# Layer 2's last node stage made block by block inside its second edge pass

## The reference, cut to what matters

```
for i in range(LAYERS):                               # LAYERS = 2
    x1 = _gat_layer(x1, src, dst, W, a_s, a_d, concat=i != LAYERS - 1)   # 8 heads, softmax over edges
    x2 = _rel_gcn_layer(x2, src, dst, edge_weight, gcn_params[i])        # relu of a weighted mean
return jnp.maximum(x1, x2)
...
h = jnp.maximum(_layernorm(x), 0.0)
x = x + _L2_gnn_ref(h, ...)
h = jnp.maximum(_layernorm(x), 0.0)
x = x + _L3_gnn_ref(h, ...)       # 9 steps h <- norm * A h, summed with softmax weights, then a product
```

## Time and profile before

| | us |
|---|---|
| median of 3 runs | 2660.73 |
| lowest, highest | 2654.13, 2671.45 |
| the profiled execution, its own time | 2652.48 |
| its span | 2650.7 |
| granted TensorE clock, mean over the span | 0.783 of full |
| busy: PE, DVE, ACT, POOL | 2346.3, 1452.3, 1208.4, 1198.2 |

### The profile page before, as it was taken

One profiled execution on the slowest core, in us unless ns is written; L12 is line 12 of the kernel. 1 busy time (PEld: TensorE's weight loads), 2 busy tenths in 40 slices (PEclk: granted clock), 3 DMA queues, 4 the chain that ended last, 5 costly groups with the idle time before them and its releaser, 6 DMA issues.

```text
span 2650.7 us, 51792 instructions
## 1 busy us (share of the span) xinstructions
PE 2346.3 (89%) x12833; PEld 1958.4 (74%) x12833; DVE 1452.3 (55%) x6161; ACT 1208.4 (46%) x5256; POOL 1198.2 (45%) x1268
## 2 busy tenths in 40 slices
PE   3778778787549999999899999999979999999998
PEld 2555556554339999999857777777878899888887
DVE  5656556578536666666436566665564333344443
ACT  3666667675313333333314343343674444444443
POOL 3777777700067777775077777775131000000000
PEclk9856566588755555555698697888899999999999
DMA  3242442431244444443244344443272000000002
GB/s 90 61 125 64 123 125 64 125 103 42 66 111 113 110 109 108 109 110 106 53 110 110 100 111 108 109 108 85 68 283 83 14 22 18 25 25 25 25 25 61
DMA packets 172291, 227.45 MB, mean 86 GB/s; under 512 B 63503, under 2 KB 131160, under 8 KB 171736
## 3 DMA queue, kind: packets, MB, share of 16 engines
q0 software_dynamic: 50176, 131.74, 18.8%
q1 hardware_dynamic: 114350, 88.60, 11.1%
q10 hardware_dynamic: 7466, 3.73, 0.5%
HBM read 183.63 MB, written 40.29 MB: 84 GB/s over the span
## 4 chain that ended last, share of the span: by engine, by line
PE 71%; issue 7%; DVE 7%; POOL 5%; ACT 4%; DMA 4%; ACTq 2%; DVEq 0%; SPq 0%; POOLq 0%
PE banks L2644 10%; PE banks L2640 10%; PE banks L1675 7%; PE banks L1733 7%; PE banks L1734 6%; POOL arena L229 5%; PE banks L1736 4%; PE banks L1739 3%; PE banks L2646 3%; PE banks L733 2%; PE banks L945 2%; PE banks L1737 2%; DMA arena<-h_table,arena 2%; PE banks L736 2%; PE banks L1691 1%
## 5 line engine op out<-in xcount | busy, mean ns | idle before, releaser
L229 POOL DMA_INDIRECT arena<-value_table,arena x392 | 387.2, 988 | 318.2 <-DMA ed_table<-arena 199.1
L2640 PE MATMUL banks<-counts,u_parts 128*128 128x448 f32 x1323 | 491.7, 372 | 9.6 <-DVE u_parts L2771 9.6
L2644 PE MATMUL banks<-counts_even,u_parts 128*128 128x448 f32 x1323 | 486.3, 368 | 0.0
L229 POOL DMA_INDIRECT arena<-gat_table,arena x392 | 392.2, 1001 | 207.3 <-issue 88.0
L229 POOL DMA_INDIRECT arena<-h_table,arena x392 | 376.3, 960 | 119.4 <-issue 88.4
L2819 DVE CAST counts_even<-counts 128x448 fp32r<-128x448 bf16 x450 | 163.9, 393 | 304.1 <-PE banks L2644 276.1
L733 PE MATMUL banks<-arena 128*128 128x425 bf16 x392 | 198.3, 506 | 84.6 <-ACT arena L789 77.5
L2640 PEld LDWEIGHTS banks<-counts,u_parts 128*128 128x128 f32 x1323 | 249.6, 189 | 30.3 <-issue 9.7
L736 PEld LDWEIGHTS banks<-arena 128*128 128x128 f32 x784 | 211.1, 293 | 80.9 <-issue 72.7
L2644 PEld LDWEIGHTS banks<-counts_even,u_parts 128*128 128x128 f32 x1323 | 249.5, 189 | 20.7 <-ACT counts_even L2747 0.2
L1675 PE MATMUL banks<-arena 128*128 128x256 bf16 (+1 forms) x967 | 262.8, 370 | 1.7 <-DVE arena L2250 1.7
(11 more groups left out here) (301 smaller groups left out, 4758.5 us busy)
## 6 DMA issues: line engine op xcount, KB each, us to landing
adj_rows<-arena SPq DMA_DIRECT2D x5, 4000.0 KB
counts<-adj_rows SPq DMA_DIRECT2D x2, 7200.0 KB, 21.6
arena<-ed_table SPq DMA_DIRECT2D x784, 0.5 KB
arena<-turned_rows SPq DMA_DIRECT2D x27, 448.0 KB, 3.4
arena<-h_table,arena POOLq DMA_INDIRECT x392
arena<-value_table,arena POOLq DMA_INDIRECT x392
arena<-gat_table,arena POOLq DMA_INDIRECT x392
counts<-adj_rows SPq DMA_DIRECT2D x2, 1600.0 KB, 6.2
```

Of the source, the lines that this page charges most:

```text
L229: return e.indirect_dma_start(into, None, table, bass.IndirectOffsetOnAxis(ap=index.bitcast(U32), axis=0))
L2640: e.matmul(banks[:, 2 * r, 0:HALFW], weight, C_odd[:, w0:w0 + HALFW], start=start, stop=stop)
L2644: x = e.matmul(banks[:, 2 * r + 1, 0:HALFW], weight, tile(n), start=start, stop=stop)
```

## The change

Blocks 0 to 22 are now made inside the second edge pass. Block b begins eight chunks after its last chunk, at c0 = block_end(b) + 8. In the seven chunks c0 to c0 + 6 the fillers are left out, and bank 7, in which they were written, takes the block's weight sums and products in three parts (three heads at c0, four at c0 + 3, one and the convolution at c0 + 5). ACT scales each part back into the accumulator's own columns (at its chunks c0 + 2, + 4, + 6), DVE turns the weight sums into factors at c0 + 2 and adds all at c0 + 8, normalization follows every fourth block. The factor 1/8 moves from the scales into the weights. x is loaded and stored four blocks at a time behind the gather ring; the normalized rows go to places in the accumulators that are no longer needed (`home`). Only blocks 23 and 24 stay in `layer2_end`. Count blocks 0, 2, ..., 12 are asked for when 20 blocks are normalized, 18 to 23 at the last edge product, the odd ones after the last block's addition, then 24, and 14 and 16 in the diffusion. `weights_t` spreads one row (the last step's) in place of ten.

```diff
@@ -1436,7 +1436,7 @@
-def layer2_edges(i, begin):
+def layer2_edges(i, begin, nodes):
...
@@ -1507,7 +1508,13 @@
     def sp(e):
         begin(e)
         first = Windows(e, FI, f"e2w_{i}")
+        if i:
+            nodes.begin_sp(e)
         for b in range(NBATCH):
+            if i:
+                for g in nodes.sp_at(b):
+                    nodes.x_store(e, g)
+                    nodes.x_load(e, g + 1)
             if b >= RE:
                 e.wait_ge(e2_bd, nb0 + b - RE + 1)
             first.load(b * BC)
...
+            for b in range(NBATCH, NBATCH + 8):
+                for g in nodes.sp_at(b):
+                    nodes.x_store(e, g)
+                    nodes.x_load(e, g + 1)
...
@@ -1637,13 +1649,27 @@
+        if i:
+            nodes.begin_dve(e)
         for p in range(NBATCH + 4):
+            if i and p == 1:
+                nodes.degrees(e)
             for q in range(SLOTS):
                 c = chunk_at.get(SLOTS * p + q)
                 if c is not None:
                     spread(c)
                     if c % PER == 1 and c > 3 * PER:
                         share(c // PER - 2)
+                    if i:
+                        for b, c0 in nodes.first.items():
+                            if c == c0 + 2:
+                                nodes.weigh(e, b)
+                            if c == c0 + 8:
+                                nodes.summed(e, b)
+                                if b % 4 == 3 and b < 20:
+                                    nodes.variances(e, b // 4)
+                            if c == c0 + 12 and b % 4 == 3 and b < 20:
+                                nodes.scales(e, b // 4)
...
@@ -1746,7 +1772,13 @@
                     busy(512, 512, 512)
                 if c is not None:
                     sums(c)
-                    busy(512, 256)
+                    if not i or c not in nodes.waiting:
+                        if i and c - 1 in nodes.waiting:
+                            nodes.bank_free(e, (c - nodes.first[0]) // BC // 2)
+                        busy(512, 256)
+                    else:
+                        for b, k in nodes.pe_at(c):
+                            nodes.products(e, b, k)
...
@@ -1830,6 +1864,14 @@
                         keep_shared(c // PER - 1)
                     if c >= 7:
                         store(c - 7)
+                    if i:
+                        for b, k in nodes.act_at(c):
+                            nodes.scaled(e, b, k)
+                        for b, c0 in nodes.first.items():
+                            if b % 4 == 3 and b < 20 and c == c0 + 10:
+                                nodes.root(e, b // 4)
+                            if b % 4 == 3 and b < 20 and c == c0 + 13:
+                                nodes.normed(e, b // 4)
...
-PIECES = [(23, 24), tuple(range(0, 18, 2)), tuple(range(1, 18, 2)) + (22,), (18, 19), (20, 21)]
-SOURCES = PIECES[1] + PIECES[2] + PIECES[0] + PIECES[3] + PIECES[4]
+PIECES = [tuple(range(0, 14, 2)), tuple(range(18, 24)), tuple(range(1, 18, 2)), (24,), (14, 16)]
...
+class EndNodes:
...
+    EARLY = NB - 2
+        self.XB = at(ring_at + 5 * BC * (2 * D + H), [NB - 20, D])
+        self.landed = (16, 16, 16, 32, 16)
+        self.first = {b: block_end(b) + 8 for b in range(self.EARLY)}
+        self.waiting = {c + k for c in self.first.values() for k in range(7)}
...
+    def products(self, e, b, part):
+        weight_sums, eight, last = self.places(b)
+        if part == 0:
+            if b == 0:
+                e.wait_ge(d_scales, 2)
+            e.wait_ge(e2_sacc, NC + block_end(b))
+            e.matmul(weight_sums, SACC[0:3 * (H + 1), b * P:(b + 1) * P], add_parts[0:3 * (H + 1), :], start=True, stop=True, skip_group_check=True)
+        elif b < self.EARLY:
+            e.wait_ge(self.copied.sem, self.copied.at(3 * b + part))
+        if part < 2:
+            for h in ((0, 1, 2), (3, 4, 5, 6))[part]:
+                x = e.matmul(eight[h], self.own(h, b), end_Wg[:, h, :], start=True, stop=True, skip_group_check=True)
+        else:
+            e.matmul(last[0], self.own(H - 1, b), end_Wg[:, H - 1, :], start=True, stop=True, skip_group_check=True)
+            x = e.matmul(last[1], self.own(H, b), end_Wc, start=True, stop=True, skip_group_check=True)
+        x.then_inc(self.product.sem, 1)
+    def bank_free(self, e, b):
+        e.wait_ge(self.copied.sem, self.copied.at(3 * b + 3))
+    def scaled(self, e, b, part):
+        weight_sums, eight, last = self.places(b)
+        SV = self.SV[b % 2]
+        e.wait_ge(self.product.sem, self.product.at(3 * b + part + 1))
+        if part == 0:
+            e.wait_ge(self.weighed.sem, self.weighed.at(b + 1))
+        if part < 2:
+            for h in ((0, 1, 2), (3, 4, 5, 6))[part]:
+                x = e.activation(self.own(h, b), eight[h], ACT.Copy, scale=SV[:, h:h + 1])
+        else:
+            e.activation(self.own(H - 1, b), last[0], ACT.Copy, scale=SV[:, H - 1:H])
+            x = e.activation(self.own(H, b), last[1], ACT.Relu, scale=SV[:, H:H + 1])
+        x.then_inc(self.copied.sem, 1)
+    def weigh(self, e, b):
+        do, settle = dve_own.do, lambda: dve_own.settle(e)
+        SV = self.SV[b % 2]
+        e.wait_ge(self.product.sem, self.product.at(3 * b + 1))
+        do(e.tensor_scalar_max(SV, self.places(b)[0], 1e-16))
+        settle()
+        e.reciprocal(SV, SV).then_inc(self.weighed.sem, 1)
+    def summed(self, e, b):
+        do, settle = dve_own.do, lambda: dve_own.settle(e)
+        g = self.span_of(b)
+        x = self.XB[:, b - self.SPANS[g][0], :]
+        heads = lambda h, n: ACC[:, h:h + n, b * P:(b + 1) * P]
+        e.wait_ge(self.copied.sem, self.copied.at(3 * b + 3))
+        for n in (4, 2, 1):
+            do(e.tensor_tensor(heads(0, n), heads(0, n), heads(n, n), ALU.add))
+            settle()
+        do(e.tensor_tensor(self.own(0, b), self.own(0, b), self.own(H, b), ALU.max))
+        e.wait_ge(self.x_in.sem, self.x_in.at(16 * (g + 1)))
+        settle()
+        e.tensor_tensor(x, x, self.own(0, b), ALU.add).then_inc(self.added.sem, 1)
+        e.wait_ge(self.added.sem, self.added.at(b + 1))
+        do(e.bn_stats(self.stats[b % 2], x))
+        settle()
+        do(e.bn_aggr(self.mv[:, b, :], self.stats[b % 2]))
...
+    def root(self, e, g):
+        b0, n = self.SPANS[g]
+        e.wait_ge(self.var.sem, self.var.at(g + 2))
+        e.activation(self.rs[:, b0:b0 + n], self.rs[:, b0:b0 + n], ACT.Sqrt).then_inc(self.std.sem, 1)
...
+    def normed(self, e, g):
+        b0, n = self.SPANS[g]
+        e.wait_ge(self.rooted.sem, self.rooted.at(g + 1))
+        for b in range(b0, b0 + n):
+            x = e.activation(self.home(b), self.XB[:, b - b0, :], ACT.Relu, bias=self.shift[:, b:b + 1], scale=self.rs[:, b:b + 1])
+        x.then_inc(self.made.sem, 1)
...
+    def begin_dve(self, e):
+        e.tensor_scalar_add(dinv2l, indeg, 1.0).then_inc(self.var.sem, 1)
+        e.wait_ge(self.weights.sem, self.weights.at(32))
+        e.tensor_scalar_mul(end_Wg, end_Wg, 1.0 / H).then_inc(d_scales, 1)
...
+    def sp_at(self, batch):
+        return [g for g in range(self.NS - 1) if (self.first[4 * g + 3] + 13) // BC + 6 == batch]
+    def pe_at(self, c):
+        return [(b, k) for b, c0 in self.first.items() for k in range(3) if c == c0 + 3 * k - k // 2]
+    def act_at(self, c):
+        return [(b, k) for b, c0 in self.first.items() for k in range(3) if c == c0 + 2 * k + 2]
+def layer2_end(ends):
+    LATE = (NB - 2, NB - 1)
+    G_LATE = ends.NS - 1
+        e.wait_ge(ends.stored.sem, ends.stored.at(16 * ends.NS))
+        def returned(j, h0, h1, s):
+            e.dma_start(halves(counts)[:, h0:h1, s, :], halves(adj_rows)[:, h0:h1, s, :]).then_inc(ends.back[j].sem, 16)
+        e.wait_ge(ends.made.sem, ends.made.at(G_LATE))
+        returned(0, 0, 7, 0)
+        e.wait_ge(e2_mm, 2 * NC)
+        e.dma_start(counts[:, words(18, 24)], adj_rows[:, words(18, 24)]).then_inc(ends.back[1].sem, 16)
+        e.wait_ge(ends.added.sem, ends.added.at(NB))
+        returned(2, 0, 9, 1)
+        ends.x_store(e, G_LATE)
+        done(e)
+            e.dma_start(counts[p:p + HALF, words(24, 25)], adj_rows[0:HALF, words(24, 25)]).then_inc(ends.back[3].sem, 16)
+        e.wait_ge(e2_ot, 2 * NBATCH)
+        e.wait_ge(e2_sum, 2 * NBATCH)
+        e.wait_ge(e2_ztc, 2 * NBATCH)
+        e.wait_ge(e2_m2, 2 * NBATCH)
+        e.wait_ge(e2_a, 2 * NBATCH)
+        for b in LATE:
+            for k in range(3):
+                ends.products(e, b, k)
+        ends.bank_free(e, NB - 1)
...
+        for b in LATE:
+            for k in range(3):
+                ends.scaled(e, b, k)
+        ends.root(e, G_LATE)
+        ends.normed(e, G_LATE)
+        for b in LATE:
+            ends.weigh(e, b)
+        for b in LATE:
+            ends.summed(e, b)
+        ends.variances(e, G_LATE)
+        ends.scales(e, G_LATE)
+    return Stage(sp=sp, act=act, dve=dve, pe=pe, done=done)
...
@@ -2571,7 +2660,8 @@
```

(19 more changed lines are left out.)

244 lines of the change are left out of this document (79 added, 165 removed).

## The result

The changed kernel takes 2788.5 us (median of 4, 2786.33 to 2805.55), the kernel before 2657.4 (2649.32 to 2671.45): ratio 1.050, 95% interval 1.044 to 1.056. The forecast was 2602. It is slower by 131 us, and the profiled executions stand in the same relation (spans 2787.7 and 2650.7, 137.0 apart).

A forecast was written before the change was run, and what follows sets the result against it. The prediction took gathers to bound the second edge pass and three engines together the last node stage. 2652.5 - 70.3 + 12 = 2594, on the median's scale 2660.7 - 58 = 2602 us; range 2582 to 2652.

The forecast's parts named there:

- What leaves the path: Layer 2's last node stage: only blocks 23 and 24 and the last normalization stay of 88.3 us; 70.3 us removed.
- T+18: First diffusion product 18 us after the last edge matmul, T; bounds T+15.5 to T+22.
- The added work: Second edge pass, per block: PE net +0.2 us, ScalarE 3.5 us, VectorE 2.9 us.
- Gathers lengthened by VectorE, +4: Second edge pass: 67 us more VectorE work lengthens GpSimd's gathers by 4 us in all (0 to 10).
- Table loads: ScalarE in the second edge pass: five roots cost ten table loads of 1.28 us, 14 us with the roots.
- as many slow stretches: Second edge pass: half-clock stretches stay as many as before; up to 16 us overflow the slack, +5 us taken.
- the pass still ends by the gathers: Second edge pass: a fast 16-chunk block takes 18.7 us, its gathers 20.5; the pass grows by 12 us together.
- the tail: End of the second edge pass: after the last gather some 28 chunks run at compute speed, +3 us (0 to 6).
- I take 1.5 us of PE standing per block: Second edge pass: PE stands 1.5 us per block in settles and waits, between 0 and 4.
- Rival 3: Second edge pass: each block's stall starts a slow stretch; at 60% slow, 25.5 us a block, about 2710; chance 0.08.
- Rival 2: Second edge pass: clock falls more often, four waiting chunks lacking fillers and products; at 35% slow about 2640; chance 0.23.
- Start, queues, count blocks, diffusion: Pass head and queues cost nothing; count blocks arrive with six microseconds of cover; diffusion stays 690 us.

The follow-up runs named there:

- e1d: The changed kernel with three 256-column zero fillers put back into each of a block's seven waiting chunks: 2781.0 us, 1.046 times the kernel before.
- the two parts of the distance: The changed kernel with weighing, products and copies moved later, summing still one slot behind the last copy: 2765.0 us; with only summing through writing four chunks later: 2723.0 us.
- e2b_holes: The kernel before with only the fillers left out in the same 161 chunks, on a slower chip: 3019.8 us against 3035.3, ratio 0.996.
- the version with both remedies: The changed kernel with all node steps moved apart and fillers in ten chunks of each block, on a quick chip: 2603.4 us, 0.978 times the kernel before.
- e9_waits_only: The kernel before with two bare VectorE waits a block at the places of weighing and summing, no work added: 2661.0 us, ratio 1.000.

## Why the prediction was wrong

- **What leaves the path**: right. T+18 (15.5 to 22) was 18.2; PE done with both blocks at about T+10, as counted.
- **The added work**: right in size. VectorE's sums and statistics take (32.5 + 6.9 + 6.8 + 6.7 + 4.2) / 23 = 2.5 us a block, 2.6 forecast; VectorE grew from 317 to 385 us over the pass, 67 forecast. PE's products are 2.6 us a block only at the full clock; they took 120 / 23 = 5.2.
- **Gathers lengthened by VectorE, +4**: wrong by sign, 989 ns after 1001. The rule on the shared port pair that the prediction quotes from the Trainium skill, "SBUF — State Buffer", so left no mark here, as the end of its range at 0 had it.
- **Table loads**: the ten of the five roots are there, and two more around the degrees' root at the head of the pass (1327.1 us), which the prediction had left out; their price is within noise.
- **The step that failed: "as many slow stretches", the term of +5 us, and with it "the pass still ends by the gathers", +12 us in sum.** The pass grew by 204.5 us: the gathers by 170.3 and the tail by 34.2, where +3 was forecast (40 chunks at a clock of 0.60 follow the last gather; 31 at 0.92 did before). The half clock covers 78% of the time, 26% before; in chunks, 293 of 392 against 72. (The prediction's 85 chunks and 160 us for the kernel before were too many: 72 and 140.) The standing itself, "I take 1.5 us of PE standing per block", was near: PE idles 44 us in the pass against 17, 1.2 us more a block. What it sets off was missed, twice. VectorE's own standing had no term: 5.7 us a block (131.6 / 23), though the text itself saw VectorE "only some two chunks ahead", and its steps stood two chunks behind their producers'. And PE's standing was taken as time lost once, although show a stall of 1.18 us that halved the clock. What followed was 14 stretches at the half clock, up to 147 us long, in which PE needs 1.95 us a chunk against the gathers' 1.29.
- **Rival 3** named this mechanism at 0.08. Its own formula nearly holds: with 18.7 us for a fast block and 30.0 for a slow one, 75% of the chunks slow gives 27.1 us a block; 685.5 / 24.5 = 28.0 was measured. Its share, 60%, was too low, and the stretches are fewer and longer than "each block's stall starts" one. **Rival 2's** cause, the chunks without a filler, is not enough by itself: filling them (e1d) gave 4 us. The argument used against both, that PE falling behind ends its starvation, was right (the logits' wait for gathered rows fell from 46.6 to 13.5 us) and of no use, as the new stalls come from VectorE.
- **Start, queues, count blocks, diffusion**: right. First gather 1.9 us later, diffusion 690.6 us, no wait for a count block.

## What to carry to other kernels

Price a consumer's place in an in-order engine by its distance from the producer's place: if the order of work runs an engine two slots ahead, a step put two chunks after its input has next to no cover, and everything queued behind it loses that lead. Price a stall of TensorE by the stretch at the half clock that may follow it, not by its own length, when the earlier trace rows or their like show that stalls of this size can do that. Where two causes may feed each other, test the remedies together as well: here, on quick chips, the fillers alone gave 4 us and the two parts of the distance 20 and 62, and all together 182.

## What the runs showed of the hardware

The chips differ far more than the runs of one chip: 2658 and 3030 us for the same kernel. On the slower ones all three gather passes are longer (in e2b_holes, whose edit leaves the first two passes as they were, the first takes 608 us from first to last gather and the second 617, where the kernel before has 494 and 505 on its chip), and there are halts of SP, VectorE, ScalarE and PE for which no releaser appears, while GpSimd goes on issuing a gather every 1.25 us. From e2b_holes, SP's queue and VectorE in order of time:

```profile
1567.10 20.43 SPq L1515 DMA_DIRECT2D arena<-ed_table  x8
...
1593.83 23.24 SPq L1515 DMA_DIRECT2D arena<-ed_table  x8
...
1602.28 0.23 DVE L1568 TENSOR_TENSOR arena<-banks,arena 128x64 f32<-128x64 f32 x1 [34.36 <-issue]
...
1619.01 3.82 SPq L1515 DMA_DIRECT2D arena<-ed_table  x8
```

Eight transfer issues take 3.82 us undisturbed and 20 to 23 in the halts. What holds the engines is open, and so is how much of the 370 us between the chips it explains; no run was aimed at it. The chips' difference hid much of the effect under study: a change that costs 127 us on one chip cost 42 to 44 on others.

A kernel of small fp32 products can keep the full clock for 400 us when PE never idles (the version with both remedies), and can fall to the half clock behind a single pause of 1.14 us. Not every such pause does it. From e9_waits_only, PE in order of time and the stretch that follows, at the full clock:

```profile
1776.28 0.30 PE L1702 MATMUL banks<-arena 128*64 128x128 f32 x1 [1.75 <-DVE arena L1570]
...
1774.00:1800.00 26.00, 21.47 (x161) 16.61 (x163) 15.92 (x82) 10.18 (x66) 19.90 (x21) 1.00 0.40 107
```

The Trainium skill, "TensorE: Matmul & The Clock Gate", section "Loop structure matters more than you think", says that a copy out of PSUM by VectorE doesn't break this, in a loop whose next products follow immediately. Here they didn't: VectorE's read of PSUM at 1410.57 broke it in two steps, since the work that PE needed next stood behind it in VectorE's order.
